# Two layer normalisations on VectorE: from one tensor and two scalars to one scalar and two tensors

## The reference

```
h = relu(layernorm(x));  x = x + gat2(elu(gat1(h, adj)), adj)      # graph attention, 4 heads x 128, then 1 head x 256
h = relu(layernorm(x));  x = x + relu(mha(h, adj)) @ Wo            # masked attention, 8 heads x 32
layernorm(x) = (x - mean) / sqrt(var + 1e-5)                       # over the 256 features
```

## Time and profile before

| | |
|---|---|
| median of 3 runs | 775.59 us (773.32 to 776.01) |
| the profiled execution | 774.69 us, of which 772.6 are the span of the trace |
| busy TensorE / its weight loads | 716.3 us (93%) / 593.4 us (77%) |
| busy VectorE | 681.4 us (88%) |
| busy ScalarE / GpSimd | 591.6 us (77%) / 515.8 us (67%) |
| L631 for norm1, 64 instructions | 49.6 us, mean 775 ns |
| L631 for norm2, 64 instructions | 38.8 us, mean 606 ns |
| L604, 128 instructions | 61.5 us, mean 481 ns |
| mean granted TensorE clock | 0.989 of full speed |

### The profile page before, as it was taken

One profiled execution on the slowest core, in us unless ns is written; L12 is line 12 of the kernel. 1 busy time (PEld: TensorE's weight loads), 2 busy tenths in 40 slices (PEclk: granted clock), 3 DMA queues, 4 the chain that ended last, 5 costly groups with the idle time before them and its releaser, 6 DMA issues.

```text
span 772.6 us, 26496 instructions
## 1 busy us (share of the span) xinstructions
PE 716.3 (93%) x8398; PEld 593.4 (77%) x8398; DVE 681.4 (88%) x2017; ACT 591.6 (77%) x1865; POOL 515.8 (67%) x733
## 2 busy tenths in 40 slices
PE   0389999999999999999999999999999999999973
PEld 0157788888888888888888888888888888788852
DVE  4758899999999999999999999999999989999873
ACT  0167888888888778888888788788888888788752
POOL 5456777676767676667667766676677767766551
PEclk9999999999999999999999999999999999999996
DMA  6111555666578566557766656766655666655464
GB/s 197 33 37 43 106 112 112 121 110 118 118 117 115 116 112 113 119 114 115 122 110 118 112 124 115 115 110 120 114 119 116 113 119 106 112 118 105 89 110 89
DMA packets 270423, 84.70 MB, mean 110 GB/s; under 512 B 242896, under 2 KB 269904, under 8 KB 270288
## 3 DMA queue, kind: packets, MB, share of 16 engines
q1 hardware_dynamic: 270288, 83.02, 57.8%
HBM read 15.86 MB, written 8.39 MB: 31 GB/s over the span
## 4 chain that ended last, share of the span: by engine, by line
PE 75%; DVE 9%; DMA 5%; issue 4%; SPq 3%; ACT 1%; POOL 1%; DVEq 0%; ACTq 0%; POOLq 0%
PE bank L815 28%; PE bank L840 11%; PE bank L986 7%; PE bank L947 6%; DMA hT<-h_split 4%; PE bank L966 3%; PE bank L929 3%; PE bank L936 3%; PE bank L866 3%; PE bank L891 2%; PE bank L889 2%; PE bank L881 2%; SPq L276 1%; DVE top L756 1%; PE bank L874 1%
## 5 line engine op out<-in xcount | busy, mean ns | idle before, releaser
L497 ACT ACTIVATE e<-bank,nmx,q_power 128x128 f32<-128x128 f32 x512 | 194.7, 481 | 5.1 <-DVE nmx L761 5.1
L372 POOL CAST e_split<-e 128x512 f16<-128x512 f32 x128 | 82.4, 643 | 118.6 <-ACT e L497 118.6
L374 POOL TENSOR_TENSOR e_split<-e,e_split 128x512 f16<-128x512 f32 x128 | 151.7, 1185 | 10.3
L840 PE MATMUL bank<-w,h1T 128*128 128x258 f32 x512 | 122.8, 382 | 0.7 <-DVE shift L599 0.7
L386 POOL TENSOR_TENSOR rstd<-var,minus_half 128x1 f32<-128x1 f32 x128 | 71.7, 560 | 66.6 <-DVE var L625 66.6
L815 PE MATMUL bank<-w_split,hT 128*128 128x260 f16 x768 | 98.2, 278 | 12.3 <-DMA hT<-h_split 11.9
L840 PEld LDWEIGHTS bank<-w,h1T 128*128 128x128 f32 x512 | 96.6, 190 | 16.6 <-DVE h1T L655 1.6
L448 ACT ACTIVATE eT<-lr,nmx 128x128 f32<-128x128 f32 x256 | 102.7, 458 | 0.8 <-DVE nmx L713 0.8
L815 PE MATMUL bank<-h2T,proj_split 128*128 128x128 f16 x1536 | 97.4, 220 | 1.6 <-DMA h2T<-h_split 1.6
L815 PEld LDWEIGHTS bank<-h2T,proj_split 128*128 128x128 f16 x1536 | 92.0, 99 | 3.7 <-DMA h2T<-h_split 2.4
L815 PEld LDWEIGHTS bank<-w_split,hT 128*128 128x128 f16 x768 | 71.1, 98 | 24.5 <-issue 7.0
(11 more groups left out here) (116 smaller groups left out, 1921.7 us busy)
## 6 DMA issues: line engine op xcount, KB each, us to landing
x_in<-in_x_dram SPq DMA_DIRECT2D x64, 128.0 KB, 2.3
out_dram<-x_out SPq DMA_DIRECT2D x64, 128.0 KB, 2.0
adj_in<-in_adj_dram SPq DMA_DIRECT2D x64, 64.0 KB, 2.5
e3T<-e_split SPq DMA_TRANSPOSE x128, 3.1
hT<-h_split SPq DMA_TRANSPOSE x64, 2.4
h2T<-h_split SPq DMA_TRANSPOSE x64, 2.5
attT<-att_split SPq DMA_TRANSPOSE x64, 2.8
w<-in_L_gnn_W_dram SPq DMA_DIRECT2D x2, 256.0 KB, 3.1
```

The lines of the kernel that those rows point to most:

```text
L372: pool.tensor_copy(e3_split[:, g.two, half, 0], e).then_inc(s[high_set], 1)
L374: pool.tensor_tensor(e3_split[:, g.two, half, 1], e, e3_split[:, g.two, half, 0], ALU.subtract).then_inc(s[low_set], 1)
L497: ins = act.activation(e3[:, g.two, h, :], S[:, h // 4, (h % 4) * N:(h % 4 + 1) * N], ACT.Exp, bias=nmx3[:, g.two, h:h + 1], scale=q_power ...
L840: ins = pe.matmul(X2[:, 0:D + 2], h1T[:, g.two, k * F:(k + 1) * F], w2[:, k, :], start=k == 0, stop=k == H - 1)
```

## The change

z is made by another instruction of VectorE. Before, it was tensor_scalar: one tensor (x) and two per-partition scalars (mean and rstd). Now it is scalar_tensor_tensor: a tensor (x), one per-partition scalar (mean) and a second tensor, which is rstd read 256 times with a step of zero. The arithmetic is the same: subtract, then multiply. Both normalisations use the function. No wait, no buffer and no order is touched.

```diff
                 done(dve, s[rstd_set], g)
                 free(dve, s[free_sem], g)
-                dve.tensor_scalar(z[:, g.two, which, :], src, mv[:, g.two, which, 0:1], rstd[:, g.two, which:which + 1],
-                                  ALU.subtract, ALU.mult).then_inc(s[z_set], 1)
+                dve.scalar_tensor_tensor(out=z[:, g.two, which, :], in0=src, scalar=mv[:, g.two, which, 0:1],
+                                         in1=rstd[:, g.two, which:which + 1].to_broadcast((128, D)),
+                                         op0=ALU.subtract, op1=ALU.mult).then_inc(s[z_set], 1)
```

## The result

The changed kernel takes 776.7 us in the median of 22 runs, and the kernel before 774.48 us in 22 runs beside it. The ratio is 1.0034 with a 95% interval of 1.0023 to 1.0045: slower by a third of a per cent. That is less than the 0.5% which the prediction held to be the least that a measurement can tell, but with 22 runs of each kernel the interval lies clear of 1. The predicted 776.2 us is near in absolute terms partly by luck, because it was built on the first three runs of before (775.59); against its base it had foreseen +0.08%, and +0.34% came. The profiled execution spans 773.8 us against 772.6.

A forecast was written before the change was run, and what follows sets the result against it. TensorE was taken to set the pace, with VectorE having little room. 56 steps x 0.00 plus 0.6 us for the ends, on the median of 775.59 us, gave 776.2 us; own range 773.0 to 779.5, whole range 771.0 to 787.0.

The forecast's parts named there:

- the slack: VectorE's low half of the attention columns (L667) can end 0.06 us later a step before TensorE's transposition load moves.
- the undisturbed step: TensorE's step between the same matmuls when nothing delays it, forecast to stay at 10.86 us.
- the ends of the kernel: Start-up and drain, where z changes its waits: bounds 0 and 1.0 us slower, 0.6 us taken.
- A z ends 0.15 us behind GpSimd in the old form and 0.28 us in the new one: Both normalisations on VectorE: a blocked z ends that far behind GpSimd's instruction; z of norm1 0.93 to 0.97 us.
- The price of a per-partition scalar: In the new z on VectorE, reading the mean adds 0.06 us to 0.41, so 0.47 us unblocked.
- z of norm2 reaches its data before L357: Second normalisation: the new z beats GpSimd's L357 in most steps, by 0.03 us, taking 0.47 us instead of 0.65.
- The rival in which L357 wins: Second normalisation: GpSimd goes first, z takes 0.78 us, TensorE loses 0.19 us a step, 786.8 us in all; chance 0.18.
- The sum of the step: VectorE and GpSimd from z of norm2 to relu_low: 0.18 us gained, 0.13 lost, end at 2.75 us as before.
- 56 x 0.00: TensorE's full stretch, about 91 to 707 us: 56 steps, each with no change in time.
- One that makes it earlier gives TensorE next to nothing: Attention columns (L667): a normalisation that lets them end earlier saves TensorE almost no time.
- the rival of the free operand: Both z: the step-zero operand doesn't hold the second port, columns 0.26 us earlier, 5 us faster, 771.2 us; chance 0.12.
- The start-up: At 24.75 us, z of norm1 holds up GpSimd's products for w2 (L345) for 0.13 us longer.

The follow-up runs named there:

- order_new: The changed kernel with norm1_apply moved on VectorE from the end of its list to right behind norm2_apply: 770.44 us, ratio 0.9949 to the kernel before.
- norm1_new: The kernel before with only the first normalisation in the new form: 780.34 us, ratio 1.0078.
- norm2_new: The kernel before with only the second normalisation in the new form: 770.89 us, ratio 0.9955.
- the best version: The kernel before with the second normalisation in the new form, the first in the old, and norm1_apply right behind norm2_apply: 768.29 us, ratio 0.9924.

## Why the prediction was right, and where it was off

The verdict (no shift that matters, and what there is on the slow side) was right, and so was the mechanism on VectorE and GpSimd, up to the end of ab_low. What failed is the step from there to TensorE: the slack, and with it the undisturbed step that was to stay at 10.86 us. It is luck that the errors stayed small in sum: the half that loses cost 6.0 us and the half that gains gave 3.5, and the forecast of 0.6 us rests wholly on the ends of the kernel, where this pair of executions shows 0.7 us lost in the start-up and 1.5 us gained in the drain.

- *A z ends 0.15 us behind GpSimd in the old form and 0.28 us in the new one.* Right: 0.28 us behind L364, behind L357 (order_new) and behind the cast. z of norm1 takes 0.93 us (norm1_new) to 0.97 (changed kernel) in the median, where 0.93 to 0.97 was stated.
- *The price of a per-partition scalar, 0.06 us.* Right in the sum: 0.47 us forecast for the unblocked z, 0.48 measured, minimum 0.469. No run varied the scalar alone.
- *z of norm2 reaches its data before L357.* Right in 62 of 64. The argument had a margin of 0.03 us, because it took the minimum of the old form, 0.376, from the first normalisation in the start-up. The z of norm2 that wins in the earlier trace rows takes 0.41, which gives 0.26 us from its start to its data against 0.20 for the new form (0.48 - 0.28). The rival in which L357 wins is out; its price was never tested.
- *The sum of the step.* Forecast 2.75 us for the end of relu_low, measured 2.76. The gain at norm2 and the loss at norm1 nearly cancel. The two halves alone, -3.5 and +6.0 us, show it; the prediction had them as 0.18 us gained and 0.13 us lost, without their separate prices.
- *The slack of L667 is 0.06 us a step.* **This is the term that was mis-sized.** It was read where the load of transpose_ab meets ab_low. The loads of transpose1, one instruction on, never start less than 0.12 us behind the end of ab_low and stand at 0.12 or 0.13 us in the undisturbed steps already in the kernel before. They had 0.01 us to spare or none. With that the term "56 x 0.00" is 56 x 0.02 = 1.1 us at most, and with the 0.6 us of the ends 1.7 us, where 2.2 to 2.6 us were measured. The 56 also counts steps that don't feel ab_low, as only 33 (before) to 42 (after) of 55 stand at the distances of 0.12, 0.13 and 0.23 us. For the rest there are the late transfers (waits for hT of 4.7 and 5.5 us in one execution each), which vary by that much from run to run; it stays open.
- *One that makes it earlier gives TensorE next to nothing.* Wrong. norm2_new made L667 0.11 us earlier and gained 3.5 us; 0.37 us earlier (the best version) gained 6. The prediction knew of the loss of 0.12 us a step on late transposed h and priced it in the rival of the free operand (5 us for 0.26 us earlier), but left it out here. Its lower bound there was misread too: eight waits can give at most 8 x 0.26 = 2.1 us, and not at least, since a wait shorter than 0.26 us gives only its own length.
- *The rival of the free broadcast operand.* Out, by the 0.28 us behind L357 and L364.
- *The start-up.* 0.13 us more for L345 forecast, 0.14 measured. In the same start-up a transfer of b1 varied by 0.46 us, so the early steps can't be told from such noise.

## What to carry to other kernels

When an instruction's time has a wide spread between minimum and median, set its end against the ends on the engine that shares its memory access before pricing another form of it: what counts is which of the two holds the access, and how long the loser streams afterwards. Moving the instruction by two places in the list was worth twice the change of form (4 us against 2.2 us, with opposite sign). A slack has to be read at every instruction that depends on the late stage or stands behind one that does (here the loads behind the one that waits), and an average loss on late transfers means that earliness is worth something even where the typical step doesn't wait.

## What the runs showed of the hardware

Both forms of z, and relu_low with two tensors from SBUF, ran one after the other with GpSimd's L357, L364 and L372 on their data: the loser ended 0.15 us (old form) or 0.28 us (new form, relu_low) behind the winner. This holds also when the second input of VectorE is one element read 256 times. It isn't shown for every instruction of GpSimd. In one place of the kernel before, relu_low (82.23 us) ran beside L402 (128 int32 elements, 81.89 to 82.56) and still took 0.42 us, ending 0.09 us behind it.

Which goes first isn't decided by the start in the trace: L357 starts 0.10 us behind z and won in 53 of 64 cases against the form with two scalars, and in none of the 62 ordinary cases against the form with one. That fits a race to the data. By the ends, the new form is at its data 0.48 - 0.28 = 0.20 us after its start, and the old one, where it wins, 0.41 - 0.15 = 0.26 us. These are estimates from the durations, and no run varied them alone.

A memset of 64 columns is busy 0.11 us and moves the chain behind it by 0.01 us, as it overlaps its neighbours. When the independent instruction between a small copy and its dependent subtraction (ab_high, ab_low) was taken away, the stage behind them started 0.14 us later. One load of TensorE that waits for VectorE holds the next ones too: in the undisturbed steps the loads of transpose1 start 0.12 to 0.13 us behind the end of ab_low, whether L874 starts 0.05 us (norm1_new) or 0.11 us (before) behind it.
